# A two-layer fp32 FFN kernel: zeros of the first dequantization loaded and gathered first, nibble transfers held behind their store, second scales behind the gates

## The chip, the cores and the metric

The kernel runs on one core of one Trainium2 chip. The metric is the device time of one execution in microseconds (us), median of several runs. PE is TensorE, DVE is VectorE, ACT is ScalarE, POOL is GpSimd, and SP is the sync engine, which here only issues transfers.

## The reference, cut to what matters

```python
# x: (8, 128, 512) fp32, so T = 1024 token rows of D = 512
def cond0(x, ids, W, Wr, A, B):               # 8 experts of rank 16
    base   = einsum('btd,od->bto', x, W)
    logits = einsum('btd,ed->bte', x, Wr) + 5 * one_hot(ids)[:, None, :]
    topw, topi = top_k(logits, 2)
    gates  = sum(one_hot(topi) * softmax(topw)[..., None], -2)
    h      = einsum('btd,erd->bter', x, A)
    return base + 2 * einsum('bter,bte,eor->bto', h, gates, B)

def dequant(qw, qz, sc, g):                   # 4-bit weights, groups of 128 rows
    return sc[g] * (nibbles(qw) - (nibbles(qz) + 1)[g])

def ffn0(y):                                  # 512 -> 2 x 1376 -> 512
    gate, up = split(y @ dequant(gu))
    return (silu(gate) * up) @ dequant(down)

x = x + ffn0(cond0(x, ids0, ...))
x = x + ffn1(cond1(x, w[ids1]))               # per-batch 512x512 weight, RMS norm,
return x                                      # then 512 -> 2 x 1792 -> 512, SiLU
```

## The kernel before, in words

Every fp32 matrix product is split: an operand is stored as a high part (rounded to fp32r, written by ACT, helper `hi`, L746) and a low part (the difference, written by DVE, helper `lo`, L1110), and PE does three products for one (high by high, high by low, low by high; `mm3`, L1670 to L1674). Activations lie transposed, features on the partitions and T = 1024 tokens in two halves of 512 columns.

Each engine runs its own list of instructions in the order in which the code writes it; all waits are on named semaphores. Nothing is reordered, so an instruction that waits holds up all that stands behind it on its engine. SP issues most loads and stores, ACT a few at the start, and POOL the gathers by a row index in SBUF (`gather`, L636).

The start, in the order of PE: the products of x with the adapter matrix A, the router and the first quarter of W, `base(m, ...)` for the four blocks of W, the transposes of the router's logits, then (after DVE has worked out the gates) the transposes of the expanded gates (`s_gTp`), `base(3, 2)`, which waits for `s_hg`, and the four `lora(m, bank)`. The four results y lie in PSUM banks 0, 4, 6 and 2 (two banks each). `y_split` of ACT (L781) writes the high part of one, `y_split` of DVE (L1229) the low part, and `y_copy` of ACT (L785) moves the result out of the banks. `gate(0)` then starts the first FFN: it writes to bank 0, so it waits for the first `y_copy`, and for each k for the k-th `y_split` of DVE.

The first FFN's gate and up weights are 11 tiles. A tile i becomes fp32 in `dequant_gu(i)` on DVE (L1245): the 4-bit values `nib`, to which `add_zeros` (L1218) has added the gathered zeros `zg`, minus 16, times the gathered `scale[j]`, where j = i // 2, so the second pair of tiles (2 and 3) needs the scales of `scales_gu(1)`. Then `w_hi(i)` on ACT and `w_lo(i)` on DVE write the parts into one of two ring slots. The zeros take a way of their own: `pz` is loaded (L484), unpacked by DVE into `zu` (L1151, L1152), stored by POOL to a DRAM table `zeros_gu` (L652, semaphore `s_zk`), and gathered from there by four gathers into `zg` (`s_zg`). The row indices `idx_gu` are worked out by DVE from the constants (L1140 to L1147, `s_idx`). The nibbles are loaded by SP in two transfers, each to 64 partitions (L488), and unpacked by `nibbles(part)` (L1211). In `add_zeros(part)` the parts of `ZERO_PARTS` are tiles 0 and 1, tiles 2 to 4, and tiles 5 to 10.

POOL's list around the change (L649 to L684) is: one scale gather of pair 0, the zeros' store, three more scale gathers, the wait for `s_zk`, four zero gathers, `scales_gu(1)`, `scales_gu(2)` (which waits for two dequantized tiles), then the block sums of tile 2.

DVE's list after the gates is: `nibbles`, the product of gates and adapter result (L1225, `s_hg`), the wait for `s_zg`, `add_zeros(0)`, and then

```python
dequant_gu(0)
dve.wait_ge(s_hghi, 1)
lo(hg_lo, hg_full, hg_hi, s_hglo)
dve.wait_ge(s_hglo, 1)
dequant_gu(1)
w_lo(0)
w_lo(1)
add_zeros(1)
dequant_gu(2)
y_split(0, 0)
```

The first FFN's down product runs in six units e = 0 to 5 (L1876 to L1896). Unit e needs `w_hi_dn(e)` of ACT and `w_lo_dn(e)` of DVE, and a ring slot that unit e - 2 has left. Meanwhile the first two weight tiles of the second FFN are split ahead of time: `pre_split(g)` on ACT (L895), which for g = 1 waits until the first tile's high part has been stored, `pre_low(g)` on DVE (L1391), and the stores on SP (L532 to L536).

## Time and profile before

| | |
|---|---|
| median of 3 runs | 445.08 us (445.05 to 445.09) |
| profiled execution, its time | 446.87 us |
| its span | 445.0 us |
| granted TensorE clock, mean | 0.999 |
| busy: PE, DVE, ACT, POOL | 99%, 78%, 49%, 42% of the span |
| DMA traffic | 79.98 MB, mean 180 GB/s |

The span is the time from the first to the last instruction of one profiled execution; that execution's own time has 1.87 us around it. The clock stood at full speed (2.4 GHz level) all through. A busy share is an average over the span; what a change in one place is worth is read from the timeline of that place.

### The profile page before, as it was taken

The page shows a single profiled execution, that of the slowest core. Times are in us where ns is not written, and L with a number is a line of the kernel's source. Part 1 is how long each engine was busy: PE and PEld are TensorE (multiplying, and loading weights), DVE is VectorE, ACT ScalarE, POOL GpSimd, SP SyncE. Part 2 cuts the span into 40 slices and gives each one's busy share as a digit, 9 for nine tenths or more (in the row PEclk, how much of TensorE's full clock was granted, in tenths as well). Part 3 has the DMA queues.
Part 4 walks back from the last instruction along what each step waited for, and adds up shares of the span by engine and source line. Part 5 has one row for each costly group of instructions (what it writes and reads, how often), then busy time and mean ns, then how long its engine had stood idle before and what let it go on. Part 6 is the DMA issues. An engine that isn't in the chain of part 4 may idle for free.

```text
span 445.0 us, 5522 instructions
## 1 busy us (share of the span) xinstructions
PE 439.0 (99%) x1954; PEld 358.4 (81%) x1954; DVE 345.0 (78%) x446; ACT 218.5 (49%) x285; POOL 187.9 (42%) x162
## 2 busy tenths in 40 slices
PE   8999899999999999999999999999999999999997
PEld 4787788888888888878888788888888888888886
DVE  4769997888876988948877678768688578999922
ACT  4413765565652212428677656556556544474200
POOL 0455997855007300900005869797997400000000
PEclk9999999999999999999999999999999999999999
DMA  8954123200007676178369616947658146886633
GB/s 278 224 194 144 49 71 118 61 13 1 1 0 246 212 294 273 69 273 320 144 212 330 261 47 216 308 146 263 200 197 278 56 153 261 334 294 183 217 107 141
DMA packets 30456, 79.98 MB, mean 180 GB/s; under 512 B 2384, under 2 KB 15840, under 8 KB 28768
## 3 DMA queue, kind: packets, MB, share of 16 engines
q1 hardware_dynamic: 26752, 68.24, 44.4%
q0 software_dynamic: 3104, 10.73, 7.8%
q10 hardware_dynamic: 576, 0.72, 0.5%
q8 instruction: 13, 0.21, 0.2%
q14 instruction: 11, 0.09, 0.1%
HBM read 58.95 MB, written 20.72 MB: 179 GB/s over the span
## 4 chain that ended last, share of the span: by engine, by line
PE 75%; DVE 9%; DMA 7%; issue 4%; POOL 3%; ACT 2%; SPq 0%; ACTq 0%; DVEq 0%; POOLq 0%
PE ps L1932 10%; PE ps L1930 10%; PE ps L1931 10%; PE ps L2045 5%; PE ps L2044 5%; PE ps L2043 5%; PE ps L1792 5%; PE ps L1791 5%; PE ps L1790 5%; PE ps L1670 3%; PE ps L1671 3%; PE ps L1674 3%; DMA zeros_gu<-zu 2%; DVE zn_dn L1263 2%; PE ps L1913 2%
## 5 line engine op out<-in xcount | busy, mean ns | idle before, releaser
L1670 PE MATMUL ps<-h_hi,ring_hi 128*128 128x512 f32 x152 | 59.4, 391 | 1.8 <-DVE h_lo L1110 1.6
L1110 DVE TENSOR_TENSOR ring_lo<-raw,ring_hi 128x1792 fp32r<-128x1792 f32 (+3 forms) x24 | 48.2, 2010 | 14.2 <-ACT ring_hi L746 14.2
L1671 PE MATMUL ps<-h_lo,ring_hi 128*128 128x512 f32 x152 | 59.2, 389 | 0.0
L1930 PE MATMUL ps<-zt_hi,ring_hi 128*128 128x512 f32 x140 | 54.6, 390 | 0.0
L1932 PE MATMUL ps<-zt_hi,ring_lo 128*128 128x512 f32 x140 | 54.5, 389 | 0.0
L1931 PE MATMUL ps<-zt_lo,ring_hi 128*128 128x512 f32 x140 | 54.5, 389 | 0.0
L746 ACT ACTIVATE ring_hi<-raw 128x1792 fp32r<-128x1792 f32 (+1 forms) x23 | 36.6, 1593 | 23.0 <-PE ps L1932 10.1
L1674 PE MATMUL ps<-h_hi,ring_lo 128*128 128x512 f32 x152 | 47.8, 389 | 0.0
L636 POOL DMA_INDIRECT scale<-in_sc_gu,idx_gu x20 | 26.9, 1347 | 24.1 <-DVE idx_dn L1147 16.0
L1670 PEld LDWEIGHTS ps<-h_hi,ring_hi 128*128 128x128 f32 x152 | 28.5, 188 | 8.6 <-issue 2.8
L1674 PEld LDWEIGHTS ps<-h_hi,ring_lo 128*128 128x128 f32 x152 | 28.5, 188 | 6.0
L1671 PEld LDWEIGHTS ps<-h_lo,ring_hi 128*128 128x128 f32 x152 | 28.5, 188 | 5.8
L1930 PEld LDWEIGHTS ps<-zt_hi,ring_hi 128*128 128x128 f32 x140 | 26.3, 188 | 5.9 <-issue 0.4
L1932 PEld LDWEIGHTS ps<-zt_hi,ring_lo 128*128 128x128 f32 x140 | 26.3, 188 | 5.4
L1931 PEld LDWEIGHTS ps<-zt_lo,ring_hi 128*128 128x128 f32 x140 | 26.3, 188 | 5.4
L666 POOL TENSOR_TENSOR raw<-raw 128x256 f32<-128x256 f32 x19 | 20.3, 1070 | 21.9 <-DVE raw L1245 11.4
L2045 PE MATMUL ps<-slot,wd 128*128 128x512 f32 (+1 forms) x73 | 27.8, 380 | 0.0
L2043 PE MATMUL ps<-slot,wd 128*128 128x512 f32 (+1 forms) x73 | 27.8, 380 | 0.0
L672 POOL TENSOR_TENSOR raw<-raw 128x256 f32<-128x256 f32 x19 | 26.1, 1372 | 2.7
L667 POOL TENSOR_TENSOR raw<-raw 128x256 f32<-128x256 f32 x19 | 24.5, 1287 | 0.0
L636 POOL DMA_INDIRECT dn_work<-in_tab_dn,idx_dn x11 | 12.7, 1155 | 24.5 <-PE ps L1792 21.5
L1518 DVE TENSOR_TENSOR res<-ps,res 128x512 f32<-128x512 f32 (+1 forms) x18 | 10.8, 642 | 15.4 <-PE ps L2045 15.3
(252 smaller groups left out, 1117.7 us busy)
## 6 DMA issues: line engine op xcount, KB each, us to landing
ad_raw<-in_w1T SPq DMA_DIRECT2D x8, 1024.0 KB, 6.2
wd<-down_weights SPq DMA_DIRECT2D x7, 1024.0 KB, 5.7
down_weights<-dhi SPq DMA_DIRECT2D x7, 896.0 KB, 4.6
down_weights<-dlo SPq DMA_DIRECT2D x7, 896.0 KB, 4.1
raw<-in_gu SPq DMA_DIRECT2D x12, 512.0 KB, 3.6
wd<-down_weights SPq DMA_DIRECT2D x7, 768.0 KB, 5.7
draw<-in_d SPq DMA_DIRECT2D x7, 512.0 KB, 4.4
dn_work<-in_qw_dn SPq DMA_DIRECT2D x11, 256.0 KB, 4.0
```

What stands on the lines that cost most here:

```text
L636: pool.indirect_dma_start(dst, None, table, bass.IndirectOffsetOnAxis(ap=index, axis=0)).then_inc(done, 16)
L672: pool.tensor_tensor(s4, a12, s2, ALU.subtract).then_inc(s_sum[4], 1)
L746: act.activation(dst, src, ACT.Copy).then_inc(done, 1)
L1110: dve.tensor_tensor(dst, src, hi_part.bitcast(F32), ALU.subtract).then_inc(done_sem, 1)
L1670: pe.matmul(ps[:, bank + hf, :], w_hi, v_hi[:, t], start=first, stop=False)
L1671: pe.matmul(ps[:, bank + hf, :], w_hi, v_lo[:, t], start=False, stop=False)
L1674: ins = pe.matmul(ps[:, bank + hf, :], w_lo, v_hi[:, t], start=False, stop=last)
L1930: pe.matmul(ps[:, bank, :], ring1_hi[s][:, w], z_hi[:, t], start=first and k == 0, stop=False, skip_group_check=True)
L1931: pe.matmul(ps[:, bank, :], ring1_hi[s][:, w], z_lo[:, t], start=False, stop=False, skip_group_check=True)
L1932: ins = pe.matmul(ps[:, bank, :], ring1_lo[s][:, w], z_hi[:, t], start=False, stop=k == 1, skip_group_check=True)
L2043: pe.matmul(ps[:, bank, c], w_hi, v_hi[:, c], start=k == LAST_K if bank != own else k == 0 and i in (1, 2, 3, 5), stop=False, skip_group_c ...
L2045: return pe.matmul(ps[:, bank, c], w_lo, v_hi[:, c], start=False, stop=k == DH - 1 or (n == 6 and m == 1 and k == LAST_K - 1), skip_group_ ...
```

## The change

The load of the packed zeros moves from SP's queue to ACT's, right behind its first load. DVE unpacks them between two early pieces of x, ahead of `x_lo(2)`. POOL stores them at once, gathers them as soon as the index is there, and only then gathers the four scale parts of pair 0; the gathers of pair 1 (`scales_gu(1)`) wait for the product of the gates (`s_hg`). SP issues the nibbles in three transfers to all 128 partitions (tiles 0 to 3, 4 to 7, 8 to 10; the host lays the 64 rows out twice), after a wait for the zeros' store. `add_zeros` has four parts instead of three, and the parts move up in DVE's list. On ACT and DVE the halves of down unit 4 move ahead of the second pre-split.

```diff
@@ -232,7 +232,7 @@
-        ZERO_PARTS = ((0, 2), (2, 5), (5, FT0))
+        ZERO_PARTS = ((0, 2), (2, 5), (5, 8), (8, FT0))
         m16 = nib.bitcast(U16).rearrange("p (i g w) -> p i g w", i=FT0, g=2 * KD)
@@ -481,11 +481,12 @@
                 load_x(i)
-            sp.dma_start(pz.bitcast(U32), a["qz_gu"]).then_inc(s_pz, 16)
             sp.dma_start(w0b_raw[:, :, :], a["w0b"]).then_inc(s_w0b, 16)
             sp.dma_start(b_raw[:, :], a["bT"]).then_inc(s_b, 16)
-            for hp in range(2):
-                sp.dma_start(nib[64 * hp:64 * hp + 64, :].bitcast(U32), a["qw_gu"]).then_inc(s_qw, 16)
+            sp.wait_ge(s_zk, 16)
+            for i0, i1 in ((0, 4), (4, 8), (8, FT0)):
+                w = slice(2 * P * i0, 2 * P * i1)
+                sp.dma_start(nib[:, w].bitcast(U32), a["qw_gu"][:, w]).then_inc(s_qw, 16)
@@ -646,12 +647,9 @@
-            pool.wait_ge(s_idx, 2)
-            scale_part(0, 0)
             pool.wait_ge(s_zu, 2)
             pool.dma_start(kept_z.rearrange("g (c w) -> (g c) w", c=16), zu.bitcast(U32)).then_inc(s_zk, 16)
-            for k in range(1, KD):
-                scale_part(0, k)
+            pool.wait_ge(s_idx, 2)
             pool.wait_ge(s_zk, 16)
@@ -679,6 +677,8 @@
+            scales_gu(0)
+            pool.wait_ge(s_hg, 1)
             scales_gu(1)
@@ -733,6 +733,7 @@
             load_aw(0)
+            act.dma_start(pz.bitcast(U32), a["qz_gu"]).then_inc(s_pz, 16)
             act.wait_ge(s_warm, 1)
@@ -906,8 +907,8 @@
             pre_split(0)
+            w_hi_dn(4)
             pre_split(1)
-            w_hi_dn(4)
             act.wait_ge(s_slo, 32)
@@ -1119,6 +1120,13 @@
+            def unpack_zeros():
+
+                dve.wait_ge(s_pz, 16)
+                zu3 = zu.bitcast(U8).rearrange("p (w e) -> p w e", e=2)
+                dve.tensor_scalar(zu3[:, :, 0], pz, 15, 15, ALU.bitwise_and, ALU.bitwise_xor).then_inc(s_zu, 1)
+                dve.tensor_scalar(zu3[:, :, 1], pz, 4, 15, ALU.logical_shift_right, ALU.bitwise_xor).then_inc(s_zu, 1)
+
             x0_rest = slice(HALF // 2, HALF)
@@ -1134,6 +1142,8 @@
                     aw_lo_part(X_SPLITS[i][1])
+                if i == 2:
+                    unpack_zeros()
                 x_lo(i)
@@ -1145,11 +1155,6 @@
             dve.tensor_copy(idx_dn[:, :], g_n[:, KD:KD + FT0]).then_inc(s_idx, 1)
-
-            dve.wait_ge(s_pz, 16)
-            zu3 = zu.bitcast(U8).rearrange("p (w e) -> p w e", e=2)
-            dve.tensor_scalar(zu3[:, :, 0], pz, 15, 15, ALU.bitwise_and, ALU.bitwise_xor).then_inc(s_zu, 1)
-            dve.tensor_scalar(zu3[:, :, 1], pz, 4, 15, ALU.logical_shift_right, ALU.bitwise_xor).then_inc(s_zu, 1)
@@ -1214,17 +1219,17 @@
                 i0, i1 = ZERO_PARTS[part]
-                dve.wait_ge(s_nib, 2 if i1 == FT0 else 1)
+                dve.wait_ge(s_nib, 2 if i1 > NIB_PARTS[0][1] else 1)
                 dve.tensor_tensor(m16[:, i0:i1], m16[:, i0:i1], zg16[:, i0:i1], ALU.add).then_inc(s_n, 1)
...
-            dve.wait_ge(s_qw, 32)
+            dve.wait_ge(s_qw, 48)
             for part in range(len(NIB_PARTS)):
                 nibbles(part)
+            dve.wait_ge(s_zg, 16 * KD)
+            add_zeros(0)
             dve.wait_ge(s_gTp, 1)
...
             dve.tensor_tensor(halves(hg_full), ps[:, 2:4, :], halves(hA_full), ALU.mult).then_inc(s_hg, 1)
-            dve.wait_ge(s_zg, 16 * KD)
-            add_zeros(0)
@@ -1312,20 +1317,21 @@
             dequant_gu(0)
+            add_zeros(1)
             dve.wait_ge(s_hghi, 1)
...
             w_lo(1)
-            add_zeros(1)
             dequant_gu(2)
+            add_zeros(2)
             y_split(0, 0)
...
             y_split(3, 2)
-            add_zeros(2)
+            add_zeros(3)
             b11, b12 = y_raw[:, 0:2, first], y_raw[:, 0:2, second]
@@ -1399,8 +1405,8 @@
                 dve.tensor_tensor(t, ps[:, 4 + 2 * m:6 + 2 * m, :], t, ALU.add).then_inc(s_res, 1)
+            w_lo_dn(4)
             pre_low(1)
-            w_lo_dn(4)
             for k in range(2):
@@ -2119,6 +2125,7 @@
     qg = pad_f(v["L0_ffn_qweight_gu"]).reshape(64, 2, FT0, P)
+    qb = np.ascontiguousarray(qg.transpose(0, 2, 1, 3)).view(np.uint8).reshape(64, FT0, 2 * P, 4).transpose(0, 1, 3, 2).reshape(64, -1).view(np.uint32)
     sg = pad_f(v["L0_ffn_scales_gu"]).reshape(G_GU, 2, FT0, P)
@@ -2146,7 +2153,7 @@
         "bT": v["L0_cond_B"].transpose(0, 2, 1).reshape(E * R, D)[:, order],
-        "qw_gu": np.ascontiguousarray(qg.transpose(0, 2, 1, 3)).view(np.uint8).reshape(64, FT0, 2 * P, 4).transpose(0, 1, 3, 2).reshape(64, -1).view(np.uint32),
+        "qw_gu": np.concatenate([qb, qb]),
         "sc_gu": sc_rows[:2 * NPAIRS].reshape(NPAIRS, 2, G_GU, 2 * P).transpose(0, 2, 1, 3).reshape(NPAIRS * G_GU, 4 * P),
```

## Rows read from the trace of the kernel before

**Rows 1.** The page, its first part: busy time of the engines.
```profile
PE 439.0 (99%) x1954; PEld 358.4 (81%) x1954; DVE 345.0 (78%) x446; ACT 218.5 (49%) x285; POOL 187.9 (42%) x162
```

**Rows 2.** Timeline of PE: start, duration, line, operation [idle before, releaser].
```profile
43.42 0.61 PE L1674 MATMUL ps<-h_hi,b_lo 128*128 128x512 f32 x2
45.66 0.47 PE L1670 MATMUL ps<-h_hi,ring_hi 128*128 128x512 f32 x1 [1.63 <-DVE h_lo L1110]
...
196.48 0.61 PE L1674 MATMUL ps<-h_hi,ring_lo 128*128 128x512 f32 x2
197.24 0.47 PE L1670 MATMUL ps<-h_hi,ring_hi 128*128 128x512 f32 x1
```

**Rows 3.** Timeline of DVE from 30 to 44 us.
```profile
30.43 1.23 DVE L1225 TENSOR_TENSOR gates<-ps,raw 128x1024 f32<-128x1024 f32 x1 [1.50 <-PE ps L1749]
34.31 0.69 DVE L1218 TENSOR_TENSOR nib<-nib,zg 128x1024 uint16<-128x1024 uint16 x1 [2.65 <-DMA zg<-zeros_gu,idx_gu]
35.03 1.28 DVE L1245 SCALAR_TENSOR_TENSOR raw<-nib,scale 128x1024 f32<-128x1024 uint8 x1
36.23 1.21 DVE L1110 TENSOR_TENSOR h_lo<-gates,h_hi 128x1024 fp32r<-128x1024 f32 x1
37.48 1.22 DVE L1245 SCALAR_TENSOR_TENSOR raw<-nib,scale 128x1024 f32<-128x1024 uint8 x1
38.62 2.44 DVE L1110 TENSOR_TENSOR ring_lo<-raw,ring_hi 128x1024 fp32r<-128x1024 f32 x2
40.98 0.98 DVE L1218 TENSOR_TENSOR nib<-nib,zg 128x1536 uint16<-128x1536 uint16 x1
41.99 1.22 DVE L1245 SCALAR_TENSOR_TENSOR raw<-nib,scale 128x1024 f32<-128x1024 uint8 x1
43.13 2.35 DVE L1110 TENSOR_TENSOR h_lo<-ps,h_hi 128x1024 fp32r<-128x1024 f32 x2
```

**Rows 4.** Timeline of DVE from 193 to 197 us.
```profile
193.93 2.02 DVE L1110 TENSOR_TENSOR pre_lo<-pre_raw,pre_hi 128x1792 fp32r<-128x1792 f32 x1 [2.87 <-ACT pre_hi L746]
195.87 1.22 DVE L1110 TENSOR_TENSOR ring_lo<-dn_work,ring_hi 128x1024 fp32r<-128x1024 f32 x1
```

**Rows 5.** Timeline of ACT from 39 to 46 us.
```profile
39.99 1.03 ACT L746 ACTIVATE h_hi<-ps 128x1024 fp32r<-128x1024 f32 x1 [0.19 <-PE ps L1674]
...
44.38 1.02 ACT L787 ACTIVATE y_raw<-ps 128x1024 f32<-128x1024 f32 x1 [2.00 <-DVE h_lo L1110]
```

**Rows 6.** The chain that ended last, in order of time: start, duration, what.
```profile
16.41 1.09 POOL scale L636
17.50 7.86 DMA zeros_gu<-zu
...
30.05 4.23 DMA zg<-zeros_gu,idx_gu
...
186.38 5.65 DMA first_weights<-pre_hi
```

**Rows 7.** Timeline of POOL: three scale gathers.
```profile
35.05 0.94 POOL L636 DMA_INDIRECT scale<-in_sc_gu,idx_gu  x1 [0.30 <-issue]
38.97 1.69 POOL L636 DMA_INDIRECT scale<-in_sc_gu,idx_gu  x1 [2.98 <-DVE raw L1245]
...
42.22 1.81 POOL L636 DMA_INDIRECT scale<-in_sc_gu,idx_gu  x1 [0.30 <-issue]
```

**Rows 8.** Tile `scale`, gathers at 35.05 and 38.97: from start to landing.
```profile
DMA to landing us min/median/max: 3.5/3.5/3.5
...
DMA to landing us min/median/max: 3.8/3.8/3.8
```

**Rows 9.** Landings of ACT's first load and of `pz`; DVE ahead of `x_lo(2)`.
```profile
DMA to landing us min/median/max: 4.1/4.1/4.1
...
DMA to landing us min/median/max: 9.3/9.3/9.3
...
9.81 1.29 DVE L1110 TENSOR_TENSOR act_lo<-res,act_hi 128x512 fp32r<-128x512 f32 x2 [2.15 <-ACT act_hi L746]
```

## The prediction

> **What bounds the kernel now.** I read the page's first part, the chain that ended last, the timeline of PE and then the timelines of DVE, ACT and POOL around the two places where PE stands still. PE is busy 439.0 of 445.0 us [rows 1], and once its first matmuls run the only visible holes are two [rows 2]. Matmuls there start 0.23 us apart. The last adapter matmul starts at 43.65 (the second of the pair at 43.42), so `gate(0)` could begin at 43.88; it begins at 45.66: **1.78 us lost**. The last matmul of down unit 3 starts at 196.71, unit 4 could begin at 196.94 and begins at 197.24: **0.30 us lost**. The most that mending both can give is 2.08 us. Between and behind them PE is dense, so an earlier or later `gate(0)` moves the end by as much; the chain between 133 and 197 us starts from a PE matmul and moves with it.
>
> Followed back from 45.66: `gate(0)` needs bank 0 copied out (`y_copy(0)`, ACT, 44.38 to 45.40 [rows 5]), that needs the first `y_split` of DVE, which starts at 43.13 [rows 3]. So PE starts 2.53 us after that `y_split`. ACT had its half ready at 41.02 [rows 5]; DVE was late, because it works in order and stood until the zeros landed at 34.28 [rows 3, 6]. The zeros were late because their store was issued at 17.50, landed at 25.36, and four gathers followed, the last issued at 30.05 [rows 6].
>
> **Zeros first.** The `pz` load goes from SP's queue to ACT's, behind one transfer; SP loses one issue, ACT gains one. A load in that place landed 4.1 us after its issue, `pz` in its old place 9.3 us [rows 9]. Issued at about 1.2 it lands between 5.3 and 10.5; I take the near neighbour, some 6. DVE's two small unpackings then fit ahead of `x_lo(2)`, before which it idles 2.15 us up to 9.81 [rows 9]. ACT's remaining loads start perhaps 0.5 us later, hidden since ACT and DVE work on the x pieces behind k=1 ahead of PE. The store is issued at about 8.2 on POOL's empty queue; with the old 7.86 us it lands at 16.1, surely not later, just when the index is ready (16.1, first gather at 16.41 [rows 6]). Four zero gathers and then four scale gathers at 1.25 us each (0.95 busy, 0.30 between [rows 7]) end at about 26.5, with some waiting at 28; landed 2.55 later, at 29 to 30.5. SP's three nibble transfers, now behind the wait for the store, are asked for from 16 at the latest and by about 17.5; even with the 9.3 us of `pz` the last lands at 26.8, in time for DVE's two nibble instructions ahead of the product at 30.43, and SP has nothing else behind the wait before the down weights. Cost nothing. So `add_zeros(0)` fits ahead of 30.43, and neither the gates' product nor `dequant_gu(0)` waits.
>
> **DVE's new order.** Start-to-start steps from [rows 3]: product 1.14 to 1.2, dequant 1.14, `add_zeros` of three tiles 1.01, `h_lo` of the gates 1.25 with its own wait, each `w_lo` 1.2. From 30.43: `dequant_gu(0)` 31.6, `add_zeros(1)` 32.7, `h_lo` 33.7 to 34.94, `dequant_gu(1)` 34.96, `w_lo(0)` 36.1, `w_lo(1)` 37.3 to 38.5, and `dequant_gu(2)` could start at 38.5. With `add_zeros(2)` the `y_split` would be reached at 40.7, before ACT's 41.02. This is the promise of the change: no hole at 43.88.
>
> **Second scales behind the gates.** But `dequant_gu(2)` needs the four gathers of `scales_gu(1)`. They used to be issued while DVE waited for the zeros, the last at 35.05 [rows 7]. Now they wait for the product at 31.66, and so start at 31.93 (0.27 from release to start, as at 38.97 after DVE's end at 38.70 [rows 3, 7]), alongside a DVE that never rests. The rows show what that costs: the gather at 38.97 began within `w_lo(0)` and took 1.69; the one at 42.22 began within `dequant_gu(2)` and took 1.81. Both ended 0.9 us after the next DVE instruction began (39.8 and 43.13). The gather at 35.05, beginning together with a dequant (35.03), took 0.94 [rows 3, 7]. So a gather that starts within a DVE instruction with two SBUF inputs waits for its end and then needs 0.85 to 0.9; the next starts 0.30 later. Carried over:
> first 31.93, held by `dequant_gu(0)` to 32.7, ends 33.6; second 33.9, held by `h_lo` to 34.94, ends 35.8; third 36.1, a toss-up with `w_lo(0)` starting at 36.1: ends 37.05 or 38.2; fourth 37.35 or 38.5, in or at the end of `w_lo(1)`, ends 39.4 either way. Landing follows a gather's end by 2.1 (3.8 less 1.69) to 2.55 (3.5 less 0.95) [rows 8]: 41.5 to 41.95. I take 41.75.
>
> DVE is queued behind that wait in order: `dequant_gu(2)` 41.8, `add_zeros(2)` 42.9, `y_split(0)` 43.95, `gate(0)` at 46.48. Before it was 45.66: **+0.82 us**, bounds +0.55 and +1.05. The zeros' early arrival is eaten by the scales' late one. Behind it nothing grows: the next k of `gate(0)` come 1.4 us apart (six matmuls), and the last two `y_split` (with `dequant_gu(3)` ahead of them, 48.6 and 49.8) are ready 0.6 us before their k; the weights of tile 2 are wanted only after the 96 matmuls of tiles 0 and 1, 22 us on. On POOL `scales_gu(2)` and the sums of tile 2 are queued behind the new wait; four more gathers of 1.25 to 2.1 us with their gaps from 39.7 end by 48, so the sums keep their time within that margin.
>
> The Trainium skill, page "SBUF — State Buffer", section "Who interferes with whom", says that a VectorE tensor_tensor with both inputs in SBUF contends only with GpSimd's reads, and infers that descriptor generation needs the write side and so isn't held up by it. By that inference the four gathers would keep 0.95 us each; the two long ones above speak against it for an indirect gather, whose index lies in SBUF. What it would give is the first rival below.
>
> **Down unit 4 ahead of the second pre-split.** In the kernel before DVE idles 2.87 us up to 193.93, does `pre_low(1)` and only then unit 4's low half, 195.87 to 197.09 [rows 4]. ACT can now do the high half at 186.4, when `pre_split(0)` has ended (its store's issue, 186.38 [rows 6]) and unit 2 is done (unit 3 began 48 matmuls before 196.94, at 186.0); DVE does the low half in its idle time from 191.06. Ready at 192.3. `pre_split(1)` waits for the store to 192.2 anyway, so it isn't delayed. **-0.30 us**; bounds 0 and -0.30.
>
> **Sum.** +0.82 - 0.30 = +0.5 us. The profiled execution took 446.87 (span 445.0 and 1.87 around it) and would take 447.4; the runs' median is 445.08, 1.79 less, which I keep: **445.6 us**, own range 445.2 to 446.0.
>
> **Rivals.** (a) *The gathers run unhindered*, or the DVE's waits fall so that they slip in: starts 31.93, 33.18, 34.43, 35.68, landing at 39.2, `dequant_gu(2)` 39.2, `y_split` 41.35, `gate(0)` 43.88. Both holes closed: 445.08 - 2.08 = **443.0**. Both long gathers are against it, their small number and my reckoning to 0.1 us leave it room. It ends on the other side. 22 in 100. The inference of the Trainium skill's page "SBUF — State Buffer" would lead here. (b) *The fourth gather slips in* at 37.35 just as `w_lo(1)` starts, as the one at 35.05 did: ends 38.3, lands 40.6, `gate(0)` at 45.28, -0.38 - 0.30: **444.4**. 17 in 100; it wants a coincidence within some 0.03 us. (c) *The zeros' load is late*: DVE now waits for `pz` ahead of `x_lo(2)`. If it landed after 9.4 us, each further us would be added to PE's start on k=1; with the old 9.3 us it lands at 10.5 and unpacking ends 1.04 later than 9.81: with the main case **446.6**. It was behind all of x then and is behind one transfer now, so 9 in 100. (d) The main case a little dearer, a gather more held up by one DVE instruction: +1.2, 446.8, 7 in 100. The forecast itself: 45 in 100.
>
> **Range and chances.** To leave out no more than 2 in 10 the range goes from (a) to the main case's upper bound: 442.9 to 446.0. A difference under 0.2% (0.89 us) can't be told from none here. Faster by more: (a) and a little of (b), 0.24. Slower by more: (c), (d), 0.17. Within: 0.59.
>
> **What would show it.** DVE's timeline: `add_zeros(0)` ends before 30.4, `w_lo(1)` near 38.5, then an idle stretch of some 3 us ended by the scales' DMA, where before the zeros' DMA ended one. POOL: four scale gathers after 31.9, three of them 1.7 us or longer. PE: a hole before `gate(0)` of 2 us or more, none at unit 4. If those gathers take 0.95 us, (a) is right; if the idle stretch is under 1 us and the hole gone, my reading of the port is wrong. If x_lo(2) starts after 10, (c).

## The result, and the profile after

| | before | changed |
|---|---|---|
| median | 445.25 us (444.59 to 448.94, 13 runs) | 449.14 us (446.42 to 450.98, 13 runs) |
| ratio | | 1.0073 (95%: 1.0055 to 1.009) |
| profiled execution, its span | 446.87, 445.0 us | 446.85, 445.1 us |

The changed kernel is slower by 0.7%, outside the range of 442.9 to 446.0 (forecast 445.6). The two profiled executions differ by 0.02 us, so the loss is not in this pair of profiles at all. The 13 times of the changed kernel lie in two groups: 446.42 to 447.10 (three, granted clock 1.000), and 448.57 to 450.98 (ten, of which nine with a mean clock of 0.992 to 0.996). The profile is one of the first group. A mean of 0.996 is one stretch of 3.4 us at half clock somewhere in the execution, as three profiles below show; 0.992 would be two.

The page of the changed kernel, busy time (as [rows 1]):

```profile
PE 439.6 (99%) x1954; PEld 359.1 (81%) x1954; DVE 342.1 (77%) x447; ACT 218.6 (49%) x285; POOL 179.5 (40%) x162
```

Its timeline of PE around `gate(0)` (as [rows 2]), start, duration, line, and in brackets the idle time before and what ended it:

```profile
43.68 0.61 PE L1680 MATMUL ps<-h_hi,b_lo 128*128 128x512 f32 x2
45.49 0.47 PE L1676 MATMUL ps<-h_hi,ring_hi 128*128 128x512 f32 x1 [1.20 <-DVE h_lo L1111]
...
47.89 0.61 PE L1680 MATMUL ps<-h_hi,ring_lo 128*128 128x512 f32 x2
48.74 0.50 PE L1676 MATMUL ps<-h_hi,ring_hi 128*128 128x512 f32 x1 [0.24 <-DVE h_lo L1111]
...
196.77 0.62 PE L1680 MATMUL ps<-h_hi,ring_lo 128*128 128x512 f32 x2
197.22 0.39 PE L1676 MATMUL ps<-h_hi,ring_hi 128*128 128x512 f32 x1
```

Its timeline of DVE from 29.9 us (as [rows 3]):

```profile
29.95 0.69 DVE L1223 TENSOR_TENSOR nib<-nib,zg 128x1024 uint16<-128x1024 uint16 x1
30.69 1.22 DVE L1232 TENSOR_TENSOR gates<-ps,raw 128x1024 f32<-128x1024 f32 x1
31.83 1.22 DVE L1250 SCALAR_TENSOR_TENSOR raw<-nib,scale 128x1024 f32<-128x1024 uint8 x1
32.96 0.95 DVE L1223 TENSOR_TENSOR nib<-nib,zg 128x1536 uint16<-128x1536 uint16 x1
33.83 1.22 DVE L1111 TENSOR_TENSOR h_lo<-gates,h_hi 128x1024 fp32r<-128x1024 f32 x1
35.09 1.23 DVE L1250 SCALAR_TENSOR_TENSOR raw<-nib,scale 128x1024 f32<-128x1024 uint8 x1
36.23 2.46 DVE L1111 TENSOR_TENSOR ring_lo<-raw,ring_hi 128x1024 fp32r<-128x1024 f32 x2
40.95 1.23 DVE L1250 SCALAR_TENSOR_TENSOR raw<-nib,scale 128x1024 f32<-128x1024 uint8 x1 [2.26 <-DMA scale<-in_sc_gu,idx_gu]
...
42.96 2.35 DVE L1111 TENSOR_TENSOR h_lo<-ps,h_hi 128x1024 fp32r<-128x1024 f32 x2
45.23 2.32 DVE L1250 SCALAR_TENSOR_TENSOR raw<-nib,scale 128x1024 f32<-128x1024 uint8 x1
```

Its timeline of POOL, the four gathers behind the new wait (as [rows 7]):

```profile
32.18 1.68 POOL L637 DMA_INDIRECT scale<-in_sc_gu,idx_gu  x1 [5.37 <-DVE gates L1232]
34.17 1.70 POOL L637 DMA_INDIRECT scale<-in_sc_gu,idx_gu  x1 [0.30 <-issue]
36.18 0.96 POOL L637 DMA_INDIRECT scale<-in_sc_gu,idx_gu  x1 [0.31 <-issue]
37.44 0.95 POOL L637 DMA_INDIRECT scale<-in_sc_gu,idx_gu  x1 [0.30 <-issue]
```

What to see: the zeros are in time (`add_zeros(0)` at 29.95, ahead of the product, with no wait), the gathers start at 32.18, two of them take 1.7 us, and DVE stands 2.26 us at 40.95 for the scales. The zeros' wait of [rows 3] has been exchanged for the scales' wait. `gate(0)` could start 0.46 us behind the start of the pair at 43.68, at 44.14, and starts at 45.49: 1.35 us lost where [rows 2] shows 1.78. A second hole is new: `gate(0)` could go on at 48.35 and goes on at 48.74, because `dequant_gu(3)` takes 2.32 us instead of 1.22 beside POOL's block sums. The hole at unit 4 is gone. PE is 0.26 us later at the pair ahead of `gate(0)` (43.68 against 43.42), which is scatter of the start (43.88 in the kernel before on another chip, below): PE's first fp32 matmuls run 0.4 us and more apart until 6.6 us here, and in the profile of before they are 0.2 to 0.35 apart from 5.2 us on. With that the two profiles' spans agree.

### The profile page after: what moved, and what is told of

Its sections match the earlier page's. It is cut to its first block, busy times and chain, and to the rows that moved or that the text cites. A ratio compares the mean times of both kernels' runs of the same rounds, so it can differ in the third digit from the quotient of the medians.

```text
span 445.1 us, 5525 instructions
## 1 busy us (share of the span) xinstructions
PE 439.6 (99%) x1954; PEld 359.1 (81%) x1954; DVE 342.1 (77%) x447; ACT 218.6 (49%) x285; POOL 179.5 (40%) x162
## 4 chain that ended last, share of the span: by engine, by line
PE 95%; DVE 3%; issue 1%; DVEq 0%
PE ps L1936 10%; PE ps L1938 10%; PE ps L1937 10%; PE ps L1676 9%; PE ps L1680 9%; PE ps L1677 9%; PE ps L1796 5%; PE ps L2051 5%; PE ps L2049 5%; PE ps L1798 5%; PE ps L1797 5%; PE ps L2050 5%; PE ps L1919 2%; PE ps L1917 2%; PE ps L1918 2%; DVE raw L1250 1%
## 5 line engine op out<-in xcount | busy, mean ns | idle before, releaser
L664 POOL TENSOR_TENSOR raw<-raw 128x256 f32<-128x256 f32 x19 | 19.5, 1024 | 31.8 <-DVE raw L1250 20.3
L637 POOL DMA_INDIRECT scale<-in_sc_gu,idx_gu x20 | 24.1, 1203 | 10.9 <-issue 5.5
L670 POOL TENSOR_TENSOR raw<-raw 128x256 f32<-128x256 f32 x19 | 26.6, 1399 | 2.7
L1936 PE MATMUL ps<-ze_hi,ring_hi 128*128 128x512 f32 x56 | 22.0, 393 | 0.0
```

What stands on the lines that cost most here:

```text
L637: pool.indirect_dma_start(dst, None, table, bass.IndirectOffsetOnAxis(ap=index, axis=0)).then_inc(done, 16)
L670: pool.tensor_tensor(s4, a12, s2, ALU.subtract).then_inc(s_sum[4], 1)
L1936: pe.matmul(ps[:, bank, :], ring1_hi[s][:, w], z_hi[:, t], start=first and k == 0, stop=False, skip_group_check=True)
```

## Experiments

The runs were made on six chips, named here by letters, each time with the kernel before beside them on the same chip. The first result came from chip A. Medians in us; a range is lowest to highest; a ratio is to the kernel before on the same chip, with its 95% interval. Two engines tell each other that a step is done by counting up a semaphore; that is called an increment here.

**Chip B: the change, and two parts of it.**

> The changed kernel itself, once more. Its 13 executions so far have mean granted clocks of 1.000, 0.996 and 0.992, spans of 444.6 to 446.7 us at 1.000 and 447.2 to 449.2 us below; the profile is one at 1.000. Theory H (holes): PE's standing still around gate(0), now twice (1.2 and 0.24 us by the profile), is followed in most executions by a stretch at the lower clock level there, 44 to 56 us; expected 0.6 to 0.9% slower than before, and if the profile is one at 0.996, single windows between 44 and 56 us with matmuls 0.43 us apart instead of 0.23. Theory S (start): the stretch lies in the first 10 us, where matmuls now run slowly until 6.6 us instead of 5.2; same time, but the slow matmuls lie before 12 us. Theory C (chance): ratio near 1.000.

446.60 (446.37 to 447.25, 12 runs) beside 445.97 for before (29 runs): 1.0011 (0.9993 to 1.0029). None of the twelve lies above 447.25 or has a clock under 0.999 here. Four of the 29 of before do: 448.12 to 448.45 with a mean clock of 0.996. Over chips B to F it is 8 of 112 executions of before (448.10 to 449.68), so a stretch at half clock is not peculiar to the change. `gate(0)` starts at 45.65.

```diff
-            pool.wait_ge(s_hg, 1)
             scales_gu(1)
```

> The changed kernel without POOL's wait for the gates' product ahead of the second scales: they are gathered right behind the first, from 27.1 us, where DVE's instructions are few. Both theories: the four scales land before 34 us, DVE doesn't stand at the third dequantization, the first y split starts at 41.3 us (when ACT's half is ready) and gate(0) at 44.1 us, right behind the adapter matmuls: 1.4 us earlier than 45.5. Theory H: with the hole gone the clock stays up, all executions near a span of 443.5, so 442.9 to 443.8 us on the median, 0.4% faster than before. Theory S: 1.4 us less than the changed kernel but the clock's loss stays: about 447.5 us, slower than before. If the third dequantization's rival on POOL (the block sums) still doubles the fourth one (2.3 us) a hole of 0.5 us can stay.

445.17 (444.98 to 445.75): 0.9981 (0.9962 to 1.0). Without the wait 1.4 us less than with it; `dequant_gu(2)` starts at 38.10 without waiting.

The third run is the kernel before with this alone:

```diff
+            w_hi_dn(4)
             pre_split(1)
-            w_hi_dn(4)
...
+            w_lo_dn(4)
             pre_low(1)
-            w_lo_dn(4)
```

> The kernel before with nothing but down unit 4's two halves ahead of the second pre-split. My prediction's price: -0.30 us, 444.8 us, the hole of 0.3 us at 197 us gone, no idle of PE there. Theory H and S say nothing else. Rival: the halves delay the second pre-split and its store, and unit 5's low half becomes late: 0 to +0.5 us.

445.47: 0.999 (0.9973 to 1.0007), no difference that can be measured; the interval, -1.2 to +0.3 us, holds the forecast -0.30 too. The profile, of an execution at 444.49, has no hole at `gate(0)` either, though nothing was changed there.

**Chip C: the store first, and the block sums later.**

```diff
-            pool.wait_ge(s_idx, 2)
-            scale_part(0, 0)
             pool.wait_ge(s_zu, 2)
             pool.dma_start(kept_z.rearrange("g (c w) -> (g c) w", c=16), zu.bitcast(U32)).then_inc(s_zk, 16)
-            for k in range(1, KD):
+            pool.wait_ge(s_idx, 2)
+            for k in range(KD):
                 scale_part(0, k)
```

> The kernel before, with POOL's store of the zeros ahead of the first scale gather instead of behind it (issued near 16.6 us, first in POOL's queue). Theory V (variation): the hole of 1.78 us ahead of gate(0) that the profile of before shows is no fixed part of the kernel. That execution took 446.87 us, 1.79 more than the median of its runs, and in the profile of the unit-4 experiment (same start) the store landed after 6.1 us instead of 7.9, DVE's y split waited for nobody and PE had no hole. The spread of before (444.7 to 448.4) is the spread of the zeros' arrival. Then the earlier store takes the upper part away: median 444.8 to 445.2, spread under 1 us. Rival F (fixed): the median of before holds the hole too and only the profiled executions differ; then the median falls by the hole, to 443.5 or less. Rival N: the store's landing is set by the nibbles, which fill the DMA engines until about 24 us; then it still lands at 23 to 25 and nothing changes.

448.96 (445.41 to 450.63, 6 runs) beside 445.55: 1.0064 (1.0034 to 1.0095). A miss that no theory had: its one profile was of the 445.41 execution and shows a small hole only (`gate(0)` at 44.31, 0.26 us late), and no late increment. POOL's gathers stand 1.0 us there, from 22.95 to 23.97.

```diff
             scales_gu(1)
             scales_gu(2)
+            pool.wait_ge(s_wf, 4)
             sums_gu(2)
```

> The version without POOL's wait for the product, and with POOL's block sums of tile 2 held until the fourth dequantization is done. In the profile without the wait PE still stood 0.67 us at the third k of gate(0) (46.15 to 46.82), because the fourth dequantization took 2.30 us instead of 1.22 while POOL's sums ran. Theory: with the sums later it takes 1.22 again, the hole goes, 0.6 to 0.7 us less than without the wait alone: 444.5 us. Rival: the dequantization is slow for another reason (its output or the PSUM reads around it) and stays at 2.3; or the later sums delay tile 2's weights, wanted at 65 us, no change or worse.

447.87 (446.31 to 449.26): 1.0045 (1.002 to 1.007). `dequant_gu(3)` is back to 1.21 us and the second hole is gone, but PE stands 0.58 us at 34.26 for the gates' product, as in no profile so far; the product started at 32.98, 2.2 us after PE's last transpose (29.77 and 1.04 us).

> The changed kernel with its wait for the product, but with POOL's block sums of tile 2 held until the fourth dequantization is done. Takes away the second hole (0.6 us at the third k), leaves the first (1.4 to 1.6 us). 445.9 to 446.1 us, 0.6 less than the changed kernel on the same chip. Theory H of the clock (two holes close together let it fall): all executions stay at the upper level, also on a chip where the changed kernel falls. If single executions of 448 us and more are still there, one hole is enough or the clock's loss has another cause.

446.62 (445.84 to 448.14, 6 runs): 1.002 (0.9999 to 1.004). `gate(0)` at 45.76, `dequant_gu(3)` 1.22 us, no second hole. No execution has a clock under 1.000.

> The changed kernel once more. In the first 13 executions most had a mean granted clock of 0.996 and took 448.6 to 451.0 us; in the 12 of the first experiment none was over 447.3. If the loss belongs to the kernel (theory H) some of these are above 448 again; if it belonged to that chip or hour, none. The profile, should it be one of the slow ones, shows where the matmuls run at half rate.

450.16 (448.15 to 451.02, 6 runs): 1.0094 (1.0072 to 1.0117). That is 3.5 us over the run before it on the same chip, where 0.6 was expected. The two differ only in the later sums, and POOL comes to that wait when the gathers that matter are done; nothing in the order of work explains 3.5 us. This profile (450.49) is of the second group. POOL, DVE, PE of it, in that order:

```profile
33.05 3.69 POOL L637 DMA_INDIRECT scale<-in_sc_gu,idx_gu  x1 [6.21 <-DVE gates L1232]
37.05 0.95 POOL L637 DMA_INDIRECT scale<-in_sc_gu,idx_gu  x1 [0.30 <-issue]
```
```profile
25.20 0.23 DVE L1195 TENSOR_TENSOR gates<-gates,cst 128x64 f32<-128x64 f32 x1 [0.75 <-DVE gates L1194]
...
43.12 1.23 DVE L1250 SCALAR_TENSOR_TENSOR raw<-nib,scale 128x1024 f32<-128x1024 uint8 x1 [3.56 <-DMA scale<-in_sc_gu,idx_gu]
```
```profile
44.01 0.61 PE L1680 MATMUL ps<-h_hi,b_lo 128*128 128x512 f32 x2
47.67 0.51 PE L1676 MATMUL ps<-h_hi,ring_hi 128*128 128x512 f32 x1 [3.05 <-DVE h_lo L1111]
```

And its granted clock by windows (the figure after POOL's):

```profile
47.00:48.00 1.00, 0.33 (x2) 0.32 (x3) 1.00 (x2) 1.00 (x2) 1.00 (x3) 0.98 0.74 250
48.00:49.00 1.00, 1.00 (x4) 0.81 (x3) 1.00 (x1) 1.00 (x2) 0.86 (x2) 0.50 0.03 12
49.00:50.00 1.00, 1.00 (x4) 0.81 (x3) 1.00 (x2) 0.24 (x1) 1.00 (x1) 0.50 0.00 0
50.00:51.00 1.00, 1.00 (x4) 0.71 (x4) 1.00 (x2) 0.00 (x0) 1.00 (x3) 0.50 0.00 0
51.00:52.00 1.00, 1.00 (x5) 0.82 (x4) 1.00 (x2) 0.00 (x0) 1.00 (x2) 0.82 0.00 0
```

The first gather takes 3.69 us: it begins at 33.05 and ends 0.78 us after `dequant_gu(1)` has begun at 35.96, having sat through the rest of `dequant_gu(0)`, `add_zeros(1)` and `h_lo`. `gate(0)` could start at 44.47 and starts at 47.67, 3.20 us lost, and PE behind that works at 0.50 of its clock (the 1.2 GHz level) for three windows and at 0.82 in a fourth: 3 x 0.50 + 0.18 = 1.7 us lost. `gate(0)` comes 2.02 us later than on chip B, the clock takes 1.7, and the second hole of 0.4 vanishes: 3.3 of the 3.42 us between the two profiles (450.49 and 447.07). Of the 2.02, 0.8 is there before the gathers start (the gates' product at 31.57 instead of 30.78: 0.24 from PE's start, the rest from gaps in DVE's own chain such as the 0.75 above), and 1.25 comes from the gathers.

**Chip D: is the hole of before real, is it the gather, is it the clock?**

> The kernel before, unchanged, for a second profile of it. Theory: the profile that the prediction was made from was an unusual execution (446.87 where the median was 445.08); in most executions the zeros' store lands sooner than 7.9 us after its issue, and the 1.78 us hole ahead of gate(0) is mostly not there. Then this profile, if it reads 444.5 to 445.5, shows a hole of at most 0.5 us at gate(0) and the zeros' add starting by about 32.5. Rival: the hole is in every execution and the difference lies elsewhere; then gate(0) comes 1.5 us or more after the last adapter matmul although the time is about 445. The ratio is 1.000 by construction.

445.96 (444.75 to 446.6) beside itself at 445.5: 1.0007 (0.9992 to 1.0022). Its profile is of a 445.47 execution. DVE and PE of it:

```profile
30.89 1.23 DVE L1225 TENSOR_TENSOR gates<-ps,raw 128x1024 f32<-128x1024 f32 x1 [1.51 <-PE ps L1749]
32.03 0.68 DVE L1218 TENSOR_TENSOR nib<-nib,zg 128x1024 uint16<-128x1024 uint16 x1
```
```profile
43.88 0.62 PE L1674 MATMUL ps<-h_hi,b_lo 128*128 128x512 f32 x2
44.34 0.39 PE L1670 MATMUL ps<-h_hi,ring_hi 128*128 128x512 f32 x1
...
46.60 0.61 PE L1674 MATMUL ps<-h_hi,ring_lo 128*128 128x512 f32 x2
47.47 0.50 PE L1670 MATMUL ps<-h_hi,ring_hi 128*128 128x512 f32 x1 [0.25 <-DVE h_lo L1110]
...
195.50 0.62 PE L1674 MATMUL ps<-h_hi,ring_lo 128*128 128x512 f32 x2
195.96 0.39 PE L1670 MATMUL ps<-h_hi,ring_hi 128*128 128x512 f32 x1
```

The first zero gather started at 22.68, not at 25.61, so DVE adds the zeros with no wait and `gate(0)` follows in step. Neither the 1.78 us hole of [rows 2] nor the 0.30 us one is in it (unit 4 starts at 195.96, in step). Only a 0.41 us hole at 47.47 is, again beside a `dequant_gu(3)` of 2.27 us. Matmul for matmul against the prediction's profile: 0.46 us later before `gate(0)`, 1.32 earlier at it, 0.92 earlier behind the 0.41 us hole, 1.36 earlier behind unit 4, and 1.40 at the end.

> The changed kernel without POOL's wait for the gates' product, as before, on another chip and beside the next three. If that wait is what costs, this stays at 445.0 to 445.7 here too, with no idle of DVE on the scales' transfer. Rival (what a later run on another chip suggested): POOL's gathers now lie beside DVE's chain of small instructions that works out the gates, each held up by up to a microsecond; then the gates' product starts at 32 to 33 instead of 30.7, PE waits for it, and the time is 446.5 to 448 on this chip.

445.46 (444.9 to 446.49): 0.9999 (0.9985 to 1.0012).

```diff
-            pool.wait_ge(s_hg, 1)
-            scales_gu(1)
+            sp.wait_ge(s_hg, 1)
+            for k in range(KD):
+                sp.dma_start(scale[1][:, k, :], a["sc_gu"][G_GU + k:G_GU + k + 1, :].to_broadcast([P, 4 * P])).then_inc(s_plain, 16)
```

> The changed kernel, but the second pair's scales are fetched by four plain transfers of the same size on SP's queue, behind the same wait for the gates' product, in place of POOL's four indirect gathers (it leaves out the choice of the row: each partition gets a fixed row of the scales, so the weights of tiles 2 and 3 are scaled by other numbers). Theory, that the gathers are held up by DVE's instructions: with nothing to be held the scales land at about 35, DVE goes from w_lo(1) straight into dequant_gu(2) at 38.5, gate(0) comes within 0.3 us of the last adapter matmul, and the median is 445.0 to 445.5, 1.5 us or more under the changed kernel on the same chip. Rival, that waiting for the product is late in itself whatever fetches the scales: DVE still waits 1 us or more for the scales and the median stays over 446.5.

445.31 (444.9 to 446.17): 0.9991 (0.9977 to 1.0004). The four transfers are issued from 31.5 to 32.8 and land 3.1 to 4.0 us later; `dequant_gu(2)` starts at 38.13 and PE has no hole at `gate(0)`:

```profile
43.23 0.61 PE L1683 MATMUL ps<-h_hi,b_lo 128*128 128x512 f32 x2
43.68 0.39 PE L1679 MATMUL ps<-h_hi,ring_hi 128*128 128x512 f32 x1
```

So waiting for the product is not late in itself. Late are the gathers issued there. (The changed kernel was not run on this chip; the comparison is by the profile.)

```diff
             w_lo(0)
+            dve.wait_ge(s_whi, 2)
+            for _ in range(3):
+                own(dve.tensor_tensor(ring0_lo[1][:, 0:8 * P], raw0[1][:, 0:8 * P], ring0_hi[1][:, 0:8 * P], ALU.subtract))
             w_lo(1)
```

> The changed kernel without POOL's wait, and DVE does the low part of tile 1 three times more (the same numbers written again, 1.2 us each, 3.6 us in all) ahead of dequant_gu(2), so that gate(0) starts some 3.0 to 3.6 us late although no gather is late. Theory, that a hole of about 3 us on PE brings the granted clock down for a stretch behind it: the granted clock falls to about 0.5 for 3 to 4 us behind gate(0), the mean clock reads 0.996 or less and the time is the other kernel's of this call plus 3.2 plus about 1.7, that is 449.5 to 450.5. Rival, that the clock falls for another reason (the chip, the transfers): the clock stays at full speed behind the hole and the time is up by the hole alone, to 448.0 to 448.8.

447.83 (447.38 to 451.06, 9 runs): 1.0071 (1.0047 to 1.0096). The profile (447.78) has the hole and no fall of the clock:

```profile
43.29 0.61 PE L1682 MATMUL ps<-h_hi,b_lo 128*128 128x512 f32 x2
46.50 0.47 PE L1678 MATMUL ps<-h_hi,ring_hi 128*128 128x512 f32 x1 [2.60 <-DVE h_lo L1110]
```

The time expected for the theory, 449.5 to 450.5, was missed. The nine split: five at 447.38 to 447.83 with a mean clock of 0.999 to 1.000, four at 449.43 to 451.06 with 0.995 or 0.996. The hole is 2.75 us (46.50 against 43.75). 447.8 is 2.3 over the same kernel without the delay, 2.75 less the 0.4 us hole that vanishes; in four of nine it is 2.0 us more (449.8 against 447.8, the middles of the two groups). The theory fits some executions and the rival the others. That the four fell behind this hole is read from their mean clock alone; none of them was profiled.

**Chip E: can a gap in DVE's work let the gather in?**

> The changed kernel itself, on another chip, as the measure for the next run. By what three earlier chips showed it comes either at 446.4 to 447.2 (the first of the four late gathers takes 1.7 us, PE stands 1.6 us and then 0.6 us) or at 448.5 to 451 (the first gather takes over 3 us, PE stands some 3.2 us, and in most of these the granted clock falls behind the hole, mean 0.996). Both theories of the next run expect the same of this one.

449.74 (447.04 to 451.11, 6 runs) beside 445.64: 1.0092 (1.0057 to 1.0128). Its profile is of the one at 447.04, with gathers of 1.69 and 1.70 us.

```diff
             dequant_gu(0)
+            dve.wait_ge(s_wf, 1)
             add_zeros(1)
+            dve.wait_ge(s_n, 2)
...
             dequant_gu(1)
+            dve.wait_ge(s_wf, 2)
             w_lo(0)
+            dve.wait_ge(s_wlo, 1)
             w_lo(1)
```

> The changed kernel, in which DVE waits for its own instruction to be complete before it starts the next, at four places between dequant_gu(0) and w_lo(1). In the profile two such DVE instructions without a wait start 1.14 us apart and each lasts 1.22, so that they overlap; the one pair with a wait (h_lo of the gates, then dequant_gu(1)) starts 1.26 apart, and it is there that the long gather got through. Theory, that a gather surely gets in only where DVE has stopped: each of the four gathers takes at most 1.7 us in every execution, none of the executions lies at 449 or above, the mean clock is 1.000 in all of them, and the median is 446.3 to 447.2 whatever the run beside it shows. Rival, that it is chance for another reason (the phase of the engines, the chip): where the changed kernel comes at 449 to 450, this one does too.

447.81 (446.84 to 449.62, 12 runs): 1.005 (1.0027 to 1.0073). Three of twelve above 449 (449.42 to 449.62), against four of six without the gaps (449.31 to 451.11). The median is 1.9 us lower, but the high executions are still there, and the profile (446.92) has a gather of 1.95 us where 1.7 was the expected limit. Neither theory alone. The 1.9 can't be put down to the gaps either: on chip C an edit that does not reach these gathers took 3.5 off.

> The changed kernel without POOL's wait, a third time, beside the next run and the changed kernel. The gathers of the second pair lie ahead of 32.2 and nothing waits for them. 445.0 to 445.6, as on two chips before, whatever the changed kernel shows here. Rival: gathers beside the gates' chain delay the gates' product, 446.5 or more.

447.83 (447.03 to 449.63, 12 runs): 1.0047 (1.0025 to 1.0069), outside the expected 445.0 to 445.6. Not one of them overlaps with the same kernel on chips B and D. Chip E, PE and DVE:

```profile
29.92 1.04 PE L1754 MATMUL ps<-cst,raw 128*128 128x128 f32 x8
...
35.26 0.50 PE L1675 MATMUL ps<-act_hi,w0b_hi 128*128 128x512 f32 x1 [1.11 <-DVE gates L1231]
```
```profile
25.20 0.23 DVE L1194 TENSOR_TENSOR gates<-gates,cst 128x64 f32<-128x64 f32 x1 [0.79 <-DVE gates L1193]
...
30.78 0.68 DVE L1222 TENSOR_TENSOR nib<-nib,zg 128x1024 uint16<-128x1024 uint16 x1
33.98 1.22 DVE L1231 TENSOR_TENSOR gates<-ps,raw 128x1024 f32<-128x1024 f32 x1 [2.51 <-remote]
```

The same on chip D, where it took 445.21:

```profile
29.23 1.04 PE L1754 MATMUL ps<-cst,raw 128*128 128x128 f32 x8
```
```profile
28.75 0.69 DVE L1222 TENSOR_TENSOR nib<-nib,zg 128x1024 uint16<-128x1024 uint16 x1
30.30 1.22 DVE L1231 TENSOR_TENSOR gates<-ps,raw 128x1024 f32<-128x1024 f32 x1 [0.87 <-PE ps L1754]
```

The product waits for PE's eight transposes (and for an ACT copy that ended at 21.23). On chip D it starts 0.03 us after the last one ends (30.27). On chip E the last one ends at 30.96 and the product starts at 33.98, 3.0 us later, with nothing else to wait for: the trace has the increment of the semaphore itself at 33.95, late, and the profile, which can't put it down to anyone, writes "remote". DVE's own chain of small gate instructions has gaps of 0.4 to 0.8 us there, each ended by its own instruction before.

> As the run before, and POOL's block sums of tile 2 wait for the fourth dequantized tile, so that dequant_gu(3) takes 1.22 us instead of 2.3. If the 0.4 to 0.6 us hole at the third k of gate(0) is all that is left, this is 0.4 us under the run before it: 444.7 to 445.1, the fastest of all, and 0.1 to 0.2% under the kernel before. Rival, from its first run (447.87 on another chip): something behind gate(0) or ahead of it is made worse; then it is 1 us or more over the run before it on the same chip.

447.64 (446.74 to 449.21): 1.0042 (1.0021 to 1.0063); the product waits 2.89 us for "remote". No gain over the one before it that can be told. The profile, of an execution at 449.21, has the clock fall behind a hole of 2.2 us:

```profile
35.80 0.80 PE L1676 MATMUL ps<-act_hi,w0b_hi 128*128 128x512 f32 x1 [2.01 <-DVE gates L1232]
```

**Chip F: what brings the late increments?**

> The changed kernel without POOL's wait, as the measure for the next run on the same chip. Either 445.0 to 445.6 with the gates' product within 0.3 us of PE's last transpose and every execution below 446.6 (as on two chips), or 447.0 to 449.6 with gaps in DVE's gates chain (as on one).

447.40 (446.95 to 448.65, 6 runs) beside 445.62 (444.67 to 446.34, 11 runs): 1.0055 (1.0038 to 1.0071). The product starts 3.0 us after the last transpose (33.21 against 30.20).

```diff
-            sp.wait_ge(s_zk, 16)
-            for i0, i1 in ((0, 4), (4, 8), (8, FT0)):
-                w = slice(2 * P * i0, 2 * P * i1)
-                sp.dma_start(nib[:, w].bitcast(U32), a["qw_gu"][:, w]).then_inc(s_qw, 16)
+            for hp in range(2):
+                sp.dma_start(nib[64 * hp:64 * hp + 64, :].bitcast(U32), a["qw_gu"][64 * hp:64 * hp + 64, :]).then_inc(s_qw, 16)
```

> As the run before, but the nibbles are loaded as in the kernel before: two transfers to 64 partitions each, on SP's queue right behind the b weights, not held behind the zeros' store. Theory, that the late increments come from the nibbles' packets, which now land between 13 and 20 us together with the gathers' packets and DVE's chain: where the control takes 447 or more, this takes 445.0 to 446.0 like the kernel before, and its gates chain has no gaps. Rival, that the nibbles have no part in it: it equals the control within 0.5 us.

448.18 (447.45 to 449.45): 1.0069 (1.0051 to 1.0086); the product starts 3.4 us after the last transpose, and PE's hole there is 2.0 us, with no fall of the clock. So the nibbles' transfers do not bring the late increments. (Its median is 0.8 us over that of the run before it, where the rival said 0.5 at most; the two ranges overlap.)

> The kernel before with POOL's store of the zeros ahead of the first scale gather, a second time. It took 449.0 on one chip although its one profile showed no hole over 0.5 us. If the late increments are what the changed order of gathers brings, it is again above 448 wherever the control is above 447, and its profile shows gaps in the gates chain; on a chip where the control is at 445, it is at 445.0 to 446.0. Rival, that its own order of work costs (the zeros gathered from 24 instead of 22.7): it is above 447 on any chip, with the hole ahead of gate(0).

449.90 (447.41 to 451.98): 1.0095 (1.0063 to 1.0128). This is the kernel before with nothing moved but the store. DVE, PE, then the granted clock by windows:

```profile
34.96 1.22 DVE L1224 TENSOR_TENSOR gates<-ps,raw 128x1024 f32<-128x1024 f32 x1 [3.75 <-remote]
```
```profile
34.76 0.40 PE L1673 MATMUL ps<-act_hi,w0b_lo 128*128 128x512 f32 x1 [1.50 <-issue]
36.24 0.51 PE L1669 MATMUL ps<-act_hi,w0b_hi 128*128 128x512 f32 x1 [1.08 <-DVE gates L1224]
```
```profile
36.00:37.00 1.00, 0.76 (x3) 0.67 (x4) 0.96 (x3) 0.78 (x1) 0.00 (x0) 0.92 0.00 0
37.00:38.00 1.00, 1.00 (x3) 0.78 (x3) 1.00 (x2) 0.28 (x1) 0.00 (x0) 0.50 0.00 0
38.00:39.00 1.00, 1.00 (x4) 0.76 (x3) 1.00 (x2) 0.92 (x1) 0.00 (x0) 0.50 0.00 0
39.00:40.00 1.00, 1.00 (x4) 0.81 (x3) 0.96 (x2) 0.13 (x1) 0.00 (x0) 0.50 0.00 0
```

PE's last transpose ended at 30.60, the product starts 4.4 us later, PE does one matmul between 33.26 and 36.24, and the clock falls behind it. That one matmul waits for no semaphore, and yet PE stood 1.50 us before it (0.27 and 0.69 us near the same place in the profiles of the kernel without the wait on chips E and F): so late increments are not all that happens there. In this profile, and in those of the kernel without the wait on chips E and F, POOL issues twelve gathers with 0.30 us between them, from about 16 to 33; in the kernel before it stands 1.30 us (chip D) or 3.65 us (the prediction's profile) in the middle of them, until the zeros' store has landed. But on chip D the kernel without the wait issues the same twelve without a pause and nothing is late. In each of the six profiles in which PE's increment is late, the trace has it 1.2 to 2.0 us after the end of the last of the twelve gathers.

## Why the prediction was wrong

**The mechanism of the new wait: right, for the lower group.** POOL starts the gathers at 32.18 (forecast 31.93), the first two are held by DVE's instructions with two SBUF inputs (1.68 and 1.70 us), the last lands some 2.5 us after its end, `dequant_gu(2)` waits. Forecast 41.8, measured 40.95. The third and the fourth gather began within 0.05 us of a DVE start and slipped in with 0.96 and 0.95 us. That is rival (b), to which the prediction gave 17 in 100, and not its main case: (b) had `gate(0)` at 45.28, the main case at 46.48, measured 45.49. Plain transfers in their place remove the wait, and so does taking POOL's wait away. Rival (a) is refuted by the rows. The inference on the page "SBUF — State Buffer", section "Who interferes with whom", of the Trainium skill, that descriptor generation needs the write side and is not held up by a tensor_tensor, does not hold for these gathers: 0.95 us free, 1.70 us when begun within `h_lo`, a tensor_tensor.

**The first failed step is in the sum.** "The profiled execution took 446.87 (span 445.0 and 1.87 around it) and would take 447.4; the runs' median is 445.08, 1.79 less, which I keep". That 1.79 was no offset that every execution has. It belongs to this one, in which the zeros' store landed 7.86 us after its issue [rows 6]. The second profile of before, 1.40 us shorter, shows neither the 1.78 us hole nor the 0.30 us one at unit 4, for which the same step took a credit, and the profile with unit 4 alone changed shows no hole at `gate(0)`. All but 0.1 of the 1.40 is 1.78 and 0.4 for the two holes, less 0.46 for a later start and 0.41 for the hole beside the block sums; that 1.79 and 1.78 agree so closely is in part chance. How many executions of before have the hole is not known; two of three profiles (one of them with unit 4 changed) have not. Against such an execution the change has nothing to win and brings its own hole of 1.35: 446.85 against 445.47 in the profiles, and 446.60 against 445.17 with and without POOL's wait on chip B. (Against before on chip B it is 0.63, interval -0.3 to +1.3.) The signal was in the rows: 446.87 against three runs at 445.05 to 445.09. This step accounts for the lower group, 446.4 to 447.1 instead of 445.6.

**The second failed step is the price of a held gather.** "So a gather that starts within a DVE instruction with two SBUF inputs waits for its end and then needs 0.85 to 0.9". The one profile of the upper group has a first gather of 3.69 us, through the rest of one such instruction and two more, and `gate(0)` comes 2.0 us later than in the lower group.

**The third is a term that the sum does not have: the clock.** A hole was priced at its length. The profiles with a fall show 3.4 us at half clock, 1.7 us lost: behind a hole of 3.2 us, behind one of 2.2, and behind two of 1.7 and 1.3 with one matmul between them. Holes of 2.0 and 2.75 us were followed by none in their profiles. With a hole made by DVE alone four of nine executions have the lower mean clock and take 2.0 us more. Single executions of before had it too. The terms together give the upper group: 446.6, 2.0 for the gather and the late product, 1.7 for the clock: 450.3; measured 448.6 to 451.0. That the other nine or ten executions of the upper group are like the profiled one of chip C is argued from their times and mean clocks.

**The fourth is "Zeros first ... Cost nothing", as far as is known.** The zeros' timing was right (pz issued early, `add_zeros(0)` in time). But with the store out of the way POOL's gathers follow without a pause, and on some chips (C, E and F; not B and D) semaphore increments then come late: from DVE to itself by 0.4 to 1.0 us, from PE to DVE by 2.2 to 4.4 us in six profiles. Shown by the kernel before with only the store moved (449.90 on chip F, with the late increment in its profile; 448.96 on C, without it in the one profile taken), and by the kernel without POOL's wait (447.40 and 447.83 on F and E, 445.17 and 445.46 on B and D). These are neighbours of the changed kernel. In its own four profiles PE's increment is never late; DVE's own is in three of them (chips A, C and E, not B), by 0.4 to 0.8 us, and in the one of the upper group that put the product back by half a microsecond. What this step costs the changed kernel beyond that is open.

**The block sums.** "Behind it nothing grows" was wrong by 0.4 us: `dequant_gu(3)` doubles beside them. The second profile of before has the same hole, so it is no part of the difference to it. Letting the sums wait removes it, and without POOL's wait the gain is too small to be told (447.64 against 447.83 on E). With POOL's wait the median fell by 3.5 us on chip C (446.62 against 450.16, six runs each), for which the hole is far too small. Either the instruction that was put in shifts something that the profiles don't show, or six runs are too few to know how often a kernel falls into the upper group.

**Right:** `x_lo(2)` at 9.86 against 9.81, no delay (rival (c) fell), the nibbles and DVE's order, no hole at unit 4, though its gain could not be measured.

**Open.** What makes increments late on some chips and not on others, whether it needs the twelve gathers without a pause or only their place beside DVE's gate chain, and why PE also stands there without a wait: POOL with a pause of its own in the changed order was not tried. Whether the gather of 3.69 us was held by DVE through three instructions or by something late of the same kind is not settled: gaps in DVE's work took 1.9 us off the median on chip E, and the high executions remained. Why the later sums took 3.5 us off on chip C was not followed up. No version beat the kernel before on every chip; the best on chips B and D, the change without POOL's wait, equals it there (0.9981, 0.9999) and loses 0.5% on E and F.

## What to carry to other kernels

Before a hole in a profile is priced, compare the profiled execution's time with the median: where it is higher by about the length of the hole, the hole may belong to that execution and not to the kernel, and a second profile tells. A gather issued from POOL in a stretch where DVE works without a pause on two SBUF inputs should be counted at up to four times its free length (3.69 against 0.95 us here); put it where DVE idles, or use a plain transfer where the row is known. A hole of 2 us and more on TensorE can cost another 1.7 us of clock. Time a change that moves POOL's gathers on more than one chip: the same code differed by 3.6 us between two of them, with the kernel before within 0.5.

## What the runs showed of the hardware

- A semaphore increment by PE reached DVE 2.2 us (chip C), 3.0 and 3.5 us (E) and 3.0 to 4.4 us (F) after the instruction's end, where it is 0.03 us otherwise, while POOL issued gathers one after the other; on chips B and D the same gathers came with no delay.
- An indirect gather took 3.69 us in one profile beside back-to-back DVE instructions, 1.7 to 2.0 in the others when it began within one, 0.95 free.
- After a hole of 3.20 us on PE the granted clock was 0.50 (1.2 GHz) for three windows of 1 us and 0.82 in a fourth, and it fell for the same 3.4 us behind a hole of 2.2 us and behind two holes of 1.7 and 1.3 us. After single holes of 1.35 to 2.0 us it stayed at 1.00 in every profile. A hole of 2.75 us left the mean clock at 0.999 or more in five of nine executions and at 0.996 or less in four.
- A DVE scalar_tensor_tensor took 2.3 us instead of 1.22 while POOL's fp32 tensor_tensor instructions ran.
